# Second attention: scores made twice instead of turned probabilities, and row statistics by ScalarE's accumulators

## The chip, the core and the metric

One core of a Trainium2 chip. The metric is the device time of one execution in microseconds. The kernel is written engine by engine with explicit semaphores: TensorE (matmuls and transposes), VectorE, ScalarE, GpSimd and SyncE (which issues most DMAs) each run their own list of instructions in order.

## The reference, cut to what matters

`x` is 8 x 512 x 512, the context 8 x 120 x 512. Four layers follow each other, each added to `x`. The change is in the third, a cross attention with 16 heads of 32:

```python
x = x + _L0_xattn_ref(_layernorm(x, axis=-1), ctx_1024, ...)
x = x + _L0_ffn_ref(_layernorm(x, axis=-1), L0_ffn_rhs)
x = x + _L1_xattn_ref(_layernorm(x, axis=-1), ctx_1024, L1_xattn_w_q, L1_xattn_w_k, L1_xattn_w_v, L1_xattn_w_o)
x = x + _L1_ffn_ref(_layernorm(x, axis=-1), ...)

def _L1_xattn_ref(query, kv_source, w_q, w_k, w_v, w_o):
    q = (query @ w_q.T).reshape(B, T_q, N_HEADS, HEAD_DIM)
    k = (kv_source @ w_k.T).reshape(B, T_kv, N_HEADS, HEAD_DIM)
    v = (kv_source @ w_v.T).reshape(B, T_kv, N_HEADS, HEAD_DIM)
    scale = HEAD_DIM ** (-0.5)
    attn = jax.nn.softmax(jnp.einsum('bqhd,bkhd->bhqk', q, k) * scale, axis=-1)
    out = jnp.einsum('bhqk,bkhd->bqhd', attn, v).reshape(B, T_q, D_MODEL)
    return out @ w_o.T
```

## The kernel before

The 4096 rows are 32 tiles of 128 rows (`NT`), four tiles (`TB`) to a batch. `front` does the first two layers, `attention1` the third, `shared` and `experts` the fourth. Products are made in f16 with a high and a low half of each operand, three matmuls for one (`PASSES`); a high half is written by ScalarE (`..._high`), the low half by VectorE as the difference (`..._low`).

`attention1` is a software pipeline. In step t every engine works on several tiles, in an order that is written out by hand in its own `step(t)`. For a tile u: its own layer norm (`stats`, `aggregate` on VectorE, root and application on GpSimd), `rows_transposed`, `queries` in two halves, a store of the queries to memory (`q_rows`) and three loads that bring them back in another layout (`packed_queries`), `scores` for four chunks c of four heads each (128 rows of queries by 120 keys), `maximum`, `exps` (one Exp for each head with the negated maximum as bias and the row sum by the accumulator), `prob_transposed` (four f32 transposes a chunk), `prob_high` and `prob_low`, `outputs` (the weighted sums, 12 matmuls of 32 columns a chunk), `weighted` (times the inverse row sums), `output_transposed`, `product` (the output projection in two halves of six matmuls), `residual`, the norm of the next layer (`lg`: `gate_stats`, GpSimd's root and application), `gate_transposed`, `gate_high`, `gate_low` and `gate_logits`.

`scores` uses banks 1 and 2 of PSUM in turn, `prob_transposed` 3 and 4, `outputs` 5. Bank 6 is shared by `product` (`ps_y`) and `gate_transposed` (`ps_g`), bank 7 by the row and output transposes and the gate logits. For the shared bank 6, `product(u, 0)` waits `need(pe, s["g_lo"], u - 1)`, which is the low half of the gate transposes of tile u - 2, and `gate_transposed(u)` waits `need(pe, s["x_new"], min(u + 2, NT))`, the residual of tile u + 1. Both waits stand in both kernels. In step t these are `product(t - 3)` behind `gate_low(t - 5)`, and `gate_transposed(t - 4)` behind `residual(t - 3)`.

The last front steps and the first attention steps are woven by the table `JOIN` (which front step a half step of the attention stands behind), the last attention steps and the first pieces of the next layer by `TAIL`. In the lists of rows, L1421 is `scores`, L1435 `prob_transposed`, L1450 `outputs`, L1456 the transposes of rows, outputs and gate rows, L121 the queries, L1503 `product`, L1523 and L1525 `gate_logits`; L1353 is `exps`, L1343 `prob_high`, L1221 `maximum`, L1227 `prob_low`, L1283 `output_low`, L1299 `gate_low`, L1288 `residual`, L1235 and L1242 statistics and aggregate; L1147 is the q_rows store and L130 the loads.

## Time and profile before

| | before |
|---|---|
| median of 3 runs | 1251.64 us (1249.28 to 1256.03) |
| span of the profiled execution | 1257.6 us |
| TensorE busy | 1189.3 us (95%) |
| VectorE busy | 950.4 us (76%) |
| ScalarE busy | 708.7 us (56%) |
| GpSimd busy | 589.7 us (47%) |

The profiled execution is not one of the three timed ones; of it there is the span alone. The shares are of the whole span. The attention changed here fills about 270 to 560 us of it, so the stretches tell more than the shares. A matmul's length in the trace includes its way through the array: what one costs is the distance from its start to the next start.

### The profile page before, as it was taken

Reading aid. Unit: us, or ns where it says so; the run is one execution under the profiler, and the core shown is the slowest. Engines: PE = TensorE matmul, PEld = TensorE weight load, DVE = VectorE, ACT = ScalarE, POOL = GpSimd, SP = SyncE. Lnnn points to the kernel's source line nnn. Section 1 sums busy time; section 2 is a strip of 40 time slices with the busy share of each in tenths; the row PEclk is TensorE's granted clock in tenths of the full one; section 3 lists DMA queues with packets and bytes.
Section 4 is the critical chain, followed back from the end, with each engine's and each line's share of the span. In section 5 each row is a group of like instructions: output and inputs, shape, how many; then the busy total and the mean of one; then the engine's idle time right before and its main releaser. Section 6 shows DMA issues by size and latency. Waiting matters only on the chain.

```text
span 1257.6 us, 29419 instructions
## 1 busy us (share of the span) xinstructions
PE 1189.3 (95%) x10692; PEld 822.8 (65%) x10692; DVE 950.4 (76%) x2006; ACT 708.7 (56%) x1988; POOL 589.7 (47%) x685
## 2 busy tenths in 40 slices
PE   6888998799999999999999999999999998799996
PEld 3555665588888888786444445777777776466663
DVE  5889898899999999896677777777777775445460
ACT  4377788799899999896344322222222231365552
POOL 0047668737666667733200000445544345466744
PEclk9999999999999999999999999999999999899999
DMA  9522033134445454643870141221314320799987
GB/s 346 210 60 76 1 32 46 43 111 142 165 135 169 159 172 148 181 157 119 153 196 1 41 127 34 68 44 60 69 34 108 96 68 2 220 254 242 256 139 96
DMA packets 157567, 150.28 MB, mean 119 GB/s; under 512 B 78544, under 2 KB 111472, under 8 KB 157424
## 3 DMA queue, kind: packets, MB, share of 16 engines
q1 hardware_dynamic: 139584, 125.94, 35.5%
q0 software_dynamic: 13248, 21.15, 8.9%
q10 hardware_dynamic: 4592, 1.32, 0.6%
q8 instruction: 86, 1.41, 0.5%
q14 instruction: 57, 0.47, 0.1%
HBM read 84.93 MB, written 57.19 MB: 113 GB/s over the span
## 4 chain that ended last, share of the span: by engine, by line
PE 59%; DMA 17%; issue 8%; DVE 8%; POOL 5%; ACT 3%; ACTq 0%; SPq 0%; POOLq 0%; DVEq 0%
PE bank L121 28%; DMA lists<-att_land 14%; PE bank L1503 6%; PE bank L2125 5%; PE bank L955 4%; POOL lists L1629 4%; PE bank L1435 4%; PE bank L1456 3%; PE bank L1450 2%; PE bank L1421 2%; DMA q_rows<-att_land 1%; PE bank L1024 1%; ACT att_land L1353 1%; PE bank L872 1%; PE bank L891 1%
## 5 line engine op out<-in xcount | busy, mean ns | idle before, releaser
L1629 POOL DMA_INDIRECT lists<-att_land x128 | 134.4, 1050 | 310.7 <-DVE att_land L1770 166.8
L1353 ACT ACTIVATE att_land<-bank,att_land 128x120 f32<-128x120 f32 x512 | 178.3, 375 | 11.3 <-DVE att_land L1221 11.2
L2125 PE MATMUL bank<-att_land 128*128 128x512 f16 x768 | 177.3, 381 | 0.6 <-DVE program_logits L1304 0.6
L1952 ACT ACTIVATE att_land<-program_x 128x512 f32<-128x512 f32 x40 | 25.2, 631 | 195.2 <-DVE program_x L2094 165.1
L2125 PEld LDWEIGHTS bank<-att_land 128*128 128x128 f16 x768 | 75.4, 98 | 82.9 <-issue 2.0
L121 PE MATMUL bank<-program_xs,program_wgu 128*128 128x512 f16 x576 | 128.7, 379 | 0.6 <-DVE att_land L1729 0.6
L1353 ACT ACTIVATION_READ_ACCUMULATOR att_land<-bank,att_land 128x1 f32 x512 | 112.8, 221 | 0.0
L121 PE MATMUL bank<-att_land 128*128 128x128 f16 (+1 forms) x1560 | 101.0, 221 | 0.5 <-DVE att_land L1278 0.5
L121 PEld LDWEIGHTS bank<-program_xs,program_wgu 128*128 128x128 f16 x576 | 56.2, 98 | 67.5 <-DVE att_land L1729 1.1
L1221 DVE TENSOR_REDUCE att_land<-bank 128x4 f32<-128x480 f32 x128 | 82.4, 644 | 20.5 <-PE bank L1421 20.1
L1503 PE MATMUL bank<-att_land 128*128 128x512 f16 x384 | 93.4, 379 | 0.0
L121 PEld LDWEIGHTS bank<-att_land 128*128 128x128 f16 x1560 | 91.1, 98 | 3.6 <-DVE att_land L1278 0.7
L1227 DVE TENSOR_TENSOR att_land<-bank,att_land 120x512 f16<-120x512 f32 x128 | 86.9, 679 | 3.5 <-ACT att_land L1343 3.1
L1343 ACT ACTIVATE att_land<-bank 120x512 f16<-120x512 f32 x128 | 77.8, 610 | 19.0 <-PE bank L1435 15.7
L2132 PE MATMUL bank<-program_x 128*128 128x256 f16 x720 | 85.1, 273 | 0.0
L2294 POOL DMA_INDIRECT out_rows<-program_x,att_land x40 | 64.7, 1617 | 35.5 <-ACT program_x L2335 25.4
L121 PE MATMUL bank<-program_x 128*128 128x256 f16 (+2 forms) x504 | 80.5, 318 | 0.6 <-DVE program_x L2387 0.6
L1903 ACT ACTIVATE att_land<-att_land 128x512 f16<-128x512 f32 x64 | 40.2, 629 | 71.1 <-PE bank L2125 30.6
L1435 PE MATMUL bank<-program_ident,att_land 128*120 128x128 f32 x512 | 78.0, 275 | 1.4 <-DVE att_land L1227 1.4
L2132 PEld LDWEIGHTS bank<-program_x 128*128 128x128 f16 x720 | 70.4, 98 | 8.2
L428 POOL TENSOR_TENSOR program_x<-program_x,att_land 128x512 f32<-128x512 f32 x32 | 40.9, 1277 | 69.8 <-ACT att_land L546 69.8
L1435 PEld LDWEIGHTS bank<-program_ident,att_land 128*120 128x120 f32 x512 | 59.3, 138 | 13.7 <-issue 2.0
(305 smaller groups left out, 2817.2 us busy)
## 6 DMA issues: line engine op xcount, KB each, us to landing
att_land<-q_rows SPq DMA_DIRECT2D x96, 128.0 KB, 2.6
xn_rows<-att_land SPq DMA_DIRECT2D x37, 256.0 KB, 3.7
out_rows<-att_land SPq DMA_DIRECT2D x37, 256.0 KB, 6.4
q_rows<-att_land SPq DMA_DIRECT2D x32, 256.0 KB, 2.9
xt_tiles<-att_land SPq DMA_DIRECT2D x32, 256.0 KB, 2.1
x_rows<-program_x SPq DMA_DIRECT2D x8, 1024.0 KB, 4.8
att_land<-x_rows SPq DMA_DIRECT2D x8, 1024.0 KB, 5.6
program_xs<-xt_tiles SPq DMA_DIRECT2D x28, 256.0 KB
```

The lines of the kernel that those rows point to most:

```text
L121: last = pe.matmul(out, lhs(a, k), rhs(b, k), start=n == 0, stop=n == len(terms) - 1)
L955: last = pe.matmul(out, lhs, rhs, start=k == 0 and i == 0, stop=k == KC - 1 and i == 2)
L1221: dve.tensor_reduce(nmax[:, u % 2, c], ps_s[c % 2][:, :, :], AX.X, ALU.max, negate=True).then_inc(c4["max"], 1)
L1227: dve.tensor_tensor(pT[0:J, c, 1], ps_p[c % 2][0:J], pT[0:J, c, 0], ALU.subtract).then_inc(c4["p_lo"], 1)
L1343: act.activation(pT[0:J, c, 0], ps_p[c % 2][0:J], ACT.Copy).then_inc(c4["p_hi"], 1)
L1353: last = act.activation(prob[:, c, h, :], ps_s[c % 2][:, h, :], ACT.Exp, bias=nmax[:, u % 2, c, h:h + 1], accum_out=rsum[:, u % 2, n:n + 1])
L1435: last = pe.transpose(ps_p[c % 2][0:J, h, :], prob[:, c, h, :], g.ident[:, :])
L1503: last = pe.matmul(ps_y[:, :], oT[:, u % 2, a, k, :], g.wo1[:, b, k, :], start=k == 0 and n == 0, stop=k == KC - 1 and n == 2)
L1629: pool.indirect_dma_start(out=io["lists"], out_offset=bass.IndirectOffsetOnAxis(ap=index[:, t, k:k + 1], axis=0), in_=load[:, t, k, :], in ...
L2125: last = pe.matmul(ps_y[i][:, :], hid[:, c % 2, a, i * P:(i + 1) * P], wd[:, q, c, :], start=c == 0 and n == 0, stop=c == NC - 1 and n == 2)
L2132: last = pe.matmul(out, lhs(a, k), rhs(q, k), start=n == 0, stop=n == len(terms) - 1)
L2294: pool.indirect_dma_start(out=io["out"], out_offset=bass.IndirectOffsetOnAxis(ap=lst[:, u * CT + n, 0:1], axis=0), in_=res[:, c, n, :], in ...
```

## The change

The probabilities are no longer made in rows and turned. The scores of a chunk are made a second time with the operands swapped (`turned_scores`: 120 keys by 128 rows), into the banks that the transposes used. The negated maxima (128 x 16) are turned by one small transpose (`maxima_transposed`), copied to f16 by ScalarE (`maxima`) and brought by one DMA into a 97th row of the packed queries, against a row of ones in the keys, so that the product already holds score minus maximum. The Exp then runs on a whole chunk, once into f16 (the high half) and once in place in PSUM (`exps`), and `prob_low` takes the difference. The row sums come out of the weighted sums as a 33rd column of each head, for which the high half of the values has a column of ones (`g.vh`); head 0 has its own place in bank 7 and its own reciprocal (`inverse_sum0`) and scaling on ScalarE (`first_weighted`). The packed queries have three places instead of two. `output_high`, `output_low`, `gate_high` and `gate_low` stand half a step to a step later, and the order of all engines in a step is new.

For tiles 8 to 31, the sum of a row and the sum of its squared differences come from two ScalarE activations with accumulators (`row_sum`, `row_squares`), with three tiny GpSimd instructions, instead of VectorE's statistics and aggregate.

The core of the diff:

```diff
-    spread(sp, g.queries[:, u % 2], io["q_rows"][u], (0, 0, 1), done[u % 2])
+    spread(sp, g.queries[:, u % 3], io["q_rows"][u], (0, 0, 1), done[u % 2])
...
     LEAD, LAG = 6, 5
-    PLACE = (1, 0, 2, 3)
     SM = 7 * D + KC * HC * J
     HEAD = 5
-    ln = Norm(m, "b", g.early(0, [P, 2, D]))
+    PLACE = (1, 0, 2, 3)
+    SUMMED = 8
+    MAXROW = slice(3 * DH, 3 * DH + 1)
+    ROWS = slice(0, 3 * DH + 1)
+    ln = Norm(m, "b", g.early(7 * D, [P, 2, D]))
+    unused = g.early(9 * D, [P, 2, D], f16)
+    nmT = g.early(10 * D, [P, 2, P], f16)
     xT = g.early(2 * D, [P, 2, 2, KC, P], f16)
     qT = g.early(4 * D, [P, 2, KC, P], f16)
-    nmax = g.early(SM, [P, 2, KC, HC])
-    prob = g.early(7 * D, [P, 4, HC, J])
+    nmax = g.early(SM, [P, 2, HC, KC])
...
+            v = t - 5
+            if live(v):
+                sp.wait_ge(s["g_lo"], v + 1)
+                sp.dma_start(io["xt_tiles"][v, :, :], gT[:, v % 2].rearrange("p q k n -> p (q k n)")).then_inc(gt_out[v % 2], 16)
             u = t + 1
             if live(u):
                 sp.wait_ge(s["q_hi"], u + 1)
                 sp.wait_ge(s["q_lo"], u + 1)
                 sp.dma_start(io["q_rows"][u], qT[:, :, :, :].rearrange("p q k n -> p q (k n)")).then_inc(q_out[u % 2], 16)
+            r = t - 1
+            if live(r):
+                sp.wait_ge(s["n_ok"], r + 1)
+                need(sp, c4["t_mm"], KC * (r - 2))
+                to = g.queries[MAXROW, r % 3].rearrange("p r n -> p (r n)").rearrange("p (a n) -> p a n", n=P)
+                sp.dma_start(to, nmT[0:HEADS, r % 2, :]).then_inc(n_in[r % 2].handle, 16)
+            if live(u):
+                sp.wait_ge(q_out[u % 2], 16 * (u // 2 + 1))
+                need(sp, c4["t_mm"], KC * (u - 2))
+                need(sp, c4["s_mm"], KC * (u - 2) + 1 if u >= 2 else 0)
+                if u == 0:
+                    sp.wait_ge(f.a["sim"], NT)
+                packed_queries(sp, g, io, u, q_in)
             v = t - 4
             if live(v):
                 sp.wait_ge(lg.ok, v + 1)
                 sp.dma_start(io["xn_rows"][v * P:(v + 1) * P, :], lg.xn[:, v % 2]).then_inc(rows_out[v % 2], 16)
...
+        def mean(u):
+            if live(u) and u >= SUMMED:
+                i = u % 4
+                if u == SUMMED:
+                    pool.wait_ge(ln.aggr, SUMMED)
+                pool.wait_ge(ln.stats, u + 1)
+                pool.wait_ge(ln.ok, u - 3)
+                pool.tensor_tensor(ln.mv[:, i, 0:1], ln.st[:, i, 0:1], g.inv_d[:, :], ALU.mult).then_inc(ln.aggr, 1)
+
+        def summed_root(u):
+
+            i = u % 4
+            need(pool, squares, u + 1)
+            pool.tensor_tensor(ln.mv[:, i, 1:2], ln.st[:, i, 1:2], g.inv_d[:, :], ALU.mult).then_inc(varied.handle, 1)
+            need(pool, varied, u + 1)
+            pool.tensor_tensor(ln.ve[:, i], ln.mv[:, i, 1:2], g.eps[:, :], ALU.add).then_inc(ln.var, 1)
+            pool.wait_ge(ln.var, u + 1)
+            pool.tensor_tensor(ln.rstd[:, i], ln.ve[:, i], g.half[:, :], ALU.pow).then_inc(ln.root, 1)
...
+        def inverse_sum0(u):
+            if live(u):
+                dve.wait_ge(c4["o_mm"], KC * u + 2)
+                need(dve, of0, u - 1)
+                dve.reciprocal(rinv[:, u % 2, 0:1], ps_o0[:, DH:DH + 1]).then_inc(inv0.handle, 1)
...
-            maximum(t - 1, 3)
-            prob_low(t - 1, 0)
+            prob_low(t - 2, 1)
+            output_low(t - 3)
+            gate_low(t - 5)
             query_low(t + 1)
             rows_low(t + 2)
             yield
-            prob_low(t - 1, 1)
             maximum(t, 0)
+            logits(t - 5)
+            prob_low(t - 2, 2)
+            maximum(t, 1)
+            if t + 5 < SUMMED:
+                aggregate(ln, t + 5)
+            if t + 6 < SUMMED:
+                stats(ln, t + 6)
+            first_rows(t + 3)
+            prob_low(t - 2, 3)
+            inverse_sum0(t - 2)
+            maximum(t, 2)
+            inverse_sums(t - 2)
             weighted(t - 2)
-            logits(t - 5)
-            maximum(t, 1)
-            prob_low(t - 1, 2)
+            prob_low(t - 1, 0)
             residual(t - 3)
+            maximum(t, 3)
             gate_stats(t - 3)
-            maximum(t, 2)
-            aggregate(ln, t + 5)
-            stats(ln, t + 6)
-            first_rows(t + 3)
-            prob_low(t - 1, 3)
-            output_low(t - 2)
             aggregate(lg, t - 3)
-            gate_low(t - 4)
-            inverse_sums(t - 1)
...
+            act.activation(pT[0:J, c, 0], ps_p[c % 2][0:J], ACT.Exp)
+            act.activation(ps_p[c % 2][0:J], ps_p[c % 2][0:J], ACT.Exp).then_inc(c4["exp"], 1)
+
+        def row_sum(u):
+            if live(u) and u >= SUMMED:
+                if u == SUMMED:
+                    act.wait_ge(ln.stats, SUMMED)
+                act.wait_ge(f.q["x_new"], u + 1)
+                act.wait_ge(ln.aggr, u - 3)
+                if u > SUMMED:
+                    need(act, squares, u - 1)
+                act.activation(unused[:, u % 2], g.x[:, u, :], ACT.Copy, accum_out=ln.st[:, u % 4, 0:1]).then_inc(ln.stats, 1)
+
+        def row_squares(u):
+
+            if live(u) and u >= SUMMED:
+                act.wait_ge(ln.aggr, u + 1)
+                act.wait_ge(ln.var, u - 3)
+                act.activation(unused[:, u % 2], g.x[:, u, :], ACT.Square, scale=-1.0, bias=ln.mv[:, u % 4, 0:1],
+                               accum_out=ln.st[:, u % 4, 1:2]).then_inc(squares.handle, 1)
+
+        def maxima(u):
+            if live(u):
+                act.wait_ge(s["n_mm"], u + 1)
+                need(act, n_in[u % 2], 16 * (u // 2))
+                act.activation(nmT[0:HEADS, u % 2, :], ps_n, ACT.Copy).then_inc(s["n_ok"], 1)
...
-            prob_high(t - 1, 0)
+            exps(t - 2, 1)
+            output_high(t - 3)
+            gate_high(t - 5)
             query_high(t + 1)
             rows_high(t + 2)
             yield
-            prob_high(t - 1, 1)
-            exps(t - 1, 3)
-            prob_high(t - 1, 2)
-            exps(t, 0)
-            exps(t, 1)
-            prob_high(t - 1, 3)
-            output_high(t - 2)
-            gate_high(t - 4)
-            exps(t, 2)
+            exps(t - 2, 2)
+            maxima(t - 1)
+            exps(t - 2, 3)
+            row_squares(t + 5)
+            row_sum(t + 6)
+            first_weighted(t - 2)
+            exps(t - 1, 0)
...
+        def maxima_transposed(u):
+            if live(u):
+                pe.wait_ge(c4["max"], KC * u + KC)
+                need(pe, s["q_lo"], min(u + 3, NT))
+                pe.transpose(ps_n, nmax[:, u % 2].rearrange("p h c -> p (h c)"), g.ident[:, :]).then_inc(s["n_mm"], 1)
+
+        def turned_scores(u, c):
+
             if not live(u):
                 return
+            b = u // TB
+            if c == 0:
+                need(pe, n_in[u % 2], 16 * (u // 2 + 1))
             if u == 0 and c == 0:
+                need(pe, row_ok, 1)
                 pe.wait_ge(f.a["p_lo"], NT)
+            if u == TB and c == 0:
+                need(pe, row_ok, 2)
             if u == 0 and c == 1:
                 pe.wait_ge(f.a["y_ok"], NT)
-            pe.wait_ge(c4["exp"], KC * u + c + 1)
             need(pe, c4["p_lo"], KC * u + c - 1)
             for h in range(HC):
-                last = pe.transpose(ps_p[c % 2][0:J, h, :], prob[:, c, h, :], g.ident[:, :])
-            last.then_inc(c4["p_mm"], 1)
+                last = pe.matmul(ps_p[c % 2][0:J, h, :], g.keys[ROWS, b % 2, h, c * J:(c + 1) * J],
+                                 g.queries[ROWS, u % 3, h, c * P:(c + 1) * P], start=True, stop=True)
+            last.then_inc(c4["t_mm"], 1)
...
-            outputs(t - 2, 0)
-            outputs(t - 2, 2)
-            prob_transposed(t - 1, 0)
-            scores(t - 1, 3)
-            outputs(t - 2, 3)
+            queries(t + 1, 1)
             rows_transposed(t + 2)
-            prob_transposed(t - 1, 1)
+            turned_scores(t - 2, 2)
             scores(t, 0)
             yield
             product(t - 3, 0)
-            prob_transposed(t - 1, 2)
+            maxima_transposed(t - 1)
             gate_logits(t - 5)
+            turned_scores(t - 2, 3)
+            scores(t, 1)
+            outputs(t - 2, 1)
             queries(t + 2, 0)
-            scores(t, 1)
+            outputs(t - 2, 0)
+            scores(t, 2)
+            outputs(t - 2, 2)
+            outputs(t - 2, 3)
+            turned_scores(t - 1, 0)
             product(t - 3, 1)
-            prob_transposed(t - 1, 3)
-            outputs(t - 1, 1)
+            turned_scores(t - 1, 1)
+            scores(t, 3)
             output_transposed(t - 2)
-            scores(t, 2)
             gate_transposed(t - 4)
-            queries(t + 2, 1)
...
-        'tensor': [63, 65, 67, 67, 70, 71]}
+        'tensor': [65, 66, 67, 68, 70, 71]}
```

What this does to the order, on the two engines whose waits matter for each other. VectorE, around `gate_low` (L1299 before, L1353 after). The lines before the change are, from the top: `maximum(t, 2)`, aggregate and statistics of the own norm, `prob_low(t - 1, 3)`, `output_low(t - 2)`, aggregate of the gate norm, `gate_low(t - 4)`, the reciprocals, and the next step's `maximum`, `prob_low`, `query_low`, `rows_low`:

```order
L1221 TENSOR_REDUCE att_land<-bank 128x4
L1242 BN_AGGR attention_b_mv<-attention_b_st 128x2
L1235 BN_STATS attention_b_st<-program_x 128x6
L1227 TENSOR_TENSOR att_land<-bank,att_land 120x512
L1283 TENSOR_TENSOR att_land<-bank,att_land 128x512
L1242 BN_AGGR attention_g_mv<-attention_g_st 128x2
L1299 TENSOR_TENSOR att_land<-bank,att_land 128x512
L1261 RECIPROCAL att_land<-att_land 128x16
L1221 TENSOR_REDUCE att_land<-bank 128x4
L1227 TENSOR_TENSOR att_land<-bank,att_land 120x512
L1254 SCALAR_TENSOR_TENSOR att_land<-bank,att_land 128x512
L1278 TENSOR_TENSOR att_land<-bank,att_land 128x512
```

After the change, from `prob_low(t - 1, 0)`: `residual(t - 3)`, `maximum(t, 3)`, statistics and aggregate of the gate norm, and then the next step's `prob_low`, `output_low`, `gate_low`, `query_low`:

```order
L1276 TENSOR_TENSOR att_land<-bank,att_land 120x512
L1342 SCALAR_TENSOR_TENSOR program_x<-bank,program_x 128x512
L1270 TENSOR_REDUCE att_land<-bank 128x4
L1284 BN_STATS att_land<-program_x 128x6
L1291 BN_AGGR att_land<-att_land 128x2
L1276 TENSOR_TENSOR att_land<-bank,att_land 120x512
L1337 TENSOR_TENSOR att_land<-bank,att_land 128x512
L1353 TENSOR_TENSOR att_land<-bank,att_land 128x512
L1303 SCALAR_TENSOR_TENSOR att_land<-bank,att_land 128x512
```

The gate's low half stood at the end of the step, ahead of the next step's first instructions; now it stands behind the next step's first two, and the residual and the last maximum stand shortly ahead of it.

TensorE, from the gate transposes (into bank 6) to the first half of the output projection (L1503 before, L1608 after, into bank 6 too). Before:

```order
L1456 MATMUL bank_6<-program_ident,att_land 128x128 x4
L121 MATMUL bank_0<-att_land 128x128 x24
L1450 MATMUL bank_5<-att_land 128x32 x24
L1435 MATMUL bank_3<-program_ident,att_land 120x128 x4
L1421 MATMUL bank_2<-att_land 128x120 x4
L1450 MATMUL bank_5<-att_land 128x32 x12
L1456 MATMUL bank_7<-program_ident,att_land 128x128 x4
L1435 MATMUL bank_4<-program_ident,att_land 120x128 x4
L1421 MATMUL bank_1<-att_land 128x120 x4
L1503 MATMUL bank_6<-att_land 128x512 x6
```

After:

```order
L1531 MATMUL bank_4<-att_land 120x128 x4
L1505 MATMUL bank_2<-att_land 128x120 x4
L1562 MATMUL bank_7<-program_ident,att_land 128x128 x4
L1562 MATMUL bank_6<-program_ident,att_land 128x128 x4
L121 MATMUL bank_0<-att_land 128x128 x24
L1562 MATMUL bank_7<-program_ident,att_land 128x128 x4
L1531 MATMUL bank_3<-att_land 120x128 x4
L1505 MATMUL bank_1<-att_land 128x120 x4
L1608 MATMUL bank_6<-att_land 128x512 x6
L1513 MATMUL bank_0<-program_ident,att_land 16x128
```

Between the gate transposes and the projection stood 36 matmuls of weighted sums and two groups of probability transposes beside the queries; now the queries, one group of row transposes, one of turned scores (L1531) and one of scores are all that stands there.

## Rows read from the trace of the kernel before

**Rows 1.** Stretches: PE, PEld, DVE, ACT, POOL busy us (instructions), clock, DMA share, GB/s.

```profile
225.00:270.00 45.00, 35.84 (x480) 28.84 (x479) 38.20 (x85) 39.02 (x138) 26.16 (x40) 1.00 0.24 70
270.00:560.00 290.00, 286.97 (x4286) 248.32 (x4284) 268.82 (x528) 263.21 (x1076) 188.94 (x229) 1.00 0.49 157
560.00:612.00 52.00, 48.01 (x460) 30.27 (x459) 35.06 (x67) 29.87 (x105) 18.68 (x28) 1.00 0.45 159
```

**Rows 2.** Timeline of TensorE in one step: start, length, line, operation.

```profile
420.62 0.60 PE L1435 MATMUL bank<-program_ident,att_land 128*120 128x128 f32 x4
421.06 0.17 PE L1523 MATMUL bank<-att_land 128*128 128x18 f16 x1
...
421.26 1.50 PE L121 MATMUL bank<-att_land 128*128 128x128 f16 x24
422.60 0.38 PE L1421 MATMUL bank<-att_land 96*128 96x120 f16 x4
422.81 1.46 PE L1503 MATMUL bank<-att_land 128*128 128x512 f16 x6
...
424.54 0.46 PE L1450 MATMUL bank<-att_land 120*128 120x32 f16 x12
424.85 0.63 PE L1456 MATMUL bank<-program_ident,att_land 128*128 128x128 f32 x4
...
430.03 1.46 PE L1503 MATMUL bank<-att_land 128*128 128x512 f16 x6
431.33 0.60 PE L1435 MATMUL bank<-program_ident,att_land 128*120 128x128 f32 x4
```

**Rows 3.** Timeline of SyncE's DMA issues: q_rows stores and the loads behind one.

```profile
279.55 0.34 SPq L1147 DMA_DIRECT2D q_rows<-att_land  x1
...
409.22 0.34 SPq L1147 DMA_DIRECT2D q_rows<-att_land  x1
...
411.28 2.27 SPq L130 DMA_DIRECT2D att_land<-q_rows  x3
...
561.62 0.34 SPq L1147 DMA_DIRECT2D q_rows<-att_land  x1
```

**Rows 4.** The chain that ended last, two of its q_rows stores.

```profile
260.80 4.27 DMA q_rows<-att_land
...
332.99 7.44 DMA q_rows<-att_land
```

**Rows 5.** Timeline of ScalarE, 423 to 426 us.

```profile
423.70 0.36 ACT L1353 ACTIVATE att_land<-bank,att_land 128x120 f32<-128x120 f32 x1 [0.37 <-DVE att_land L1221]
...
424.05 0.35 ACT L1353 ACTIVATE att_land<-bank,att_land 128x120 f32<-128x120 f32 x1
...
425.06 0.61 ACT L1343 ACTIVATE att_land<-bank 120x512 f16<-120x512 f32 x1
425.54 0.62 ACT L1373 ACTIVATE att_land<-bank 128x512 f16<-128x512 f32 x1
```

**Rows 6.** Timeline of VectorE, 425 to 429 us.

```profile
425.03 0.69 DVE L1235 BATCH_NORM_STATS2 attention_g_st<-program_x 128x6 f32<-128x512 f32 x1
425.73 0.66 DVE L1221 TENSOR_REDUCE att_land<-bank 128x4 f32<-128x480 f32 x1
426.31 0.17 DVE L1242 BATCH_NORM_AGGREGATE attention_b_mv<-attention_b_st 128x2 f32<-128x6 f32 x1
...
427.56 0.68 DVE L1283 TENSOR_TENSOR att_land<-bank,att_land 128x512 f16<-128x512 f32 x1
428.16 0.17 DVE L1242 BATCH_NORM_AGGREGATE attention_g_mv<-attention_g_st 128x2 f32<-128x6 f32 x1
428.25 0.66 DVE L1299 TENSOR_TENSOR att_land<-bank,att_land 128x512 f16<-128x512 f32 x1
```

**Rows 7.** The chain of 197 to 300 us, its shares by line.

```profile
by line: PE bank L121 11.4%; issue 8.4%; PE bank L1503 7.6%; ACT att_land L1353 7.2%; DVE front_amax L768 5.3%; PE bank L1435 5.2%; PE bank L1024 4.4%; DMA q_rows<-att_land 4.1%; DVE att_land L790 3.9%; PE bank L1456 3.7%; PE bank L1450 3.4
```

**Rows 8.** A DMA issue: how many, KB each, median us to landing.

```profile
att_land<-in_gwT SPq DMA_DIRECT2D x1, 18.0 KB, 2.3
```

More of the change, by code:

```diff
@@ L212, in front @@
     rs0 = m.sb("rs0", [P, 8, 1])
-    eps4 = m.sb("eps4", [P, TB])
-    half4 = m.sb("half4", [P, TB])
-    gain4 = m.sb("gain4", [P, TB])
+    const4 = m.sb("const4", [P, 3, TB])
+    eps4, half4, gain4 = (const4[:, n] for n in range(3))
     xT = g.late(0, [P, 2, 2, KC, P], f16)
@@ L337, in shape, with landed @@
         return (slice(0, J), slice(0, D)) if kind[0] == "v" else (slice(0, P), slice(0, NH))
+    def landed(kind):
+        rows, cols = shape(kind)
+        return ps_j[rows, cols].rearrange("p (h o) -> p h o", h=HEADS) if kind == "v1" else ps_j[rows, cols]
     SPLITS = ["L0_Wv", "L1_wvT", "L1_wkT", "L1_wqT", "L1_woT"]
@@ L518, in job_high @@
                 act.wait_ge(j_mm, counted(REAL, n))
-                act.activation(hi, ps_j[rows, cols], ACT.Copy, scale=1 / WS).then_inc(j_hi, 1)
+                act.activation(hi, landed(kind), ACT.Copy, scale=1 / WS).then_inc(j_hi, 1)
         def rows_high(u):
@@ L703, in job_low @@
             else:
-                dve.scalar_tensor_tensor(lo, ps_j[rows, cols], 1 / WS, hi, ALU.mult, ALU.subtract).then_inc(j_lo, 1)
+                dve.scalar_tensor_tensor(lo, landed(kind), 1 / WS, hi, ALU.mult, ALU.subtract).then_inc(j_lo, 1)
         def statistics(u):
@@ L1183, in apply @@
                                ALU.mult).then_inc(norm.ok, 1)
-        def step(t):
+        def mean(u):
[14 more added lines that the diff above has]
+            pool.tensor_tensor(ln.rstd[:, i], ln.ve[:, i], g.half[:, :], ALU.pow).then_inc(ln.root, 1)
+        def step(t):
+            mean(t + 5)
+            if t == 0:
+                pool.wait_ge(f.j_hi, f.jobs)
+                pool.wait_ge(f.j_lo, f.jobs)
+                pool.memset(g.vh[:, :, :, DH:DH + 1], 1.0).then_inc(fixed.handle, 1)
             u = t - 4
@@ L2595, in program @@
         g.eps = m.sb("eps", [P, 1])
-        g.one = m.sb("one", [P, 1])
-        g.ws = m.sb("ws", [P, 1])
+        ones = m.sb("ones", [P, 3])
+        g.one, g.ws, g.inv_d = (ones[:, n:n + 1] for n in range(3))
         g.logits = m.sb("logits", [P, NT, E + 1])
@@ L2642, in program @@
             late = land[:, 6 * D + KN + QN + EARLY:6 * D + KN + QN + EARLY + LATE]
+            slots = land[:, 6 * D + KN:6 * D + KN + 3 * QN // 2]
             ends = 6 * D + KN + QN + EARLY + LATE
             g.v1 = g.land(ends, [P, 2, B, D], f16)
-            g.wo1 = g.land(ends + 8 * D, [P, 2, KC, D], f16)
+            g.vh = g.land(ends, [P, B, HEADS, DH + 1], f16)
+            g.vl = g.land(ends + 4 * D + VS, [P, B, D], f16)
+            g.wo1 = g.land(ends + 8 * D + VS, [P, 2, KC, D], f16)
             g.wd, g.res = g.land(ends, [P, 2, IS // P, D], f16), g.land(ends + 8 * D, [P, TB, D])
@@ L2648, in program @@
             g.keys = g.place[:, 0:KN].bitcast(f16).rearrange("p (s r n) -> p s r n", s=2, r=HC)
-            g.queries = g.place[:, KN:KN + QN].bitcast(f16).rearrange("p (s r n) -> p s r n", s=2, r=HC)
+            g.queries = slots.bitcast(f16).rearrange("p (s r n) -> p s r n", s=3, r=HC)
             g.simb, g.rs = g.place[:, KN:KN + JB], g.place[:, 2 * D:3 * D]
```

151 lines of the change are left out of this document (80 added, 71 removed).

## Prediction

> **What bounds the kernel now.** I read the busy times by stretch first, then the order and spacing of each engine inside one step, then the DMAs. The second attention runs in its pure form from about 270 to 560 us of the span. There TensorE is busy 286.97 of 290 us at full clock (1.00, the 2.4 GHz level), VectorE 268.8, ScalarE 263.2 and GpSimd 188.9 [rows 1]. The reader is to see that three engines are nearly full at once, so that work taken from one of them is worth only what the other two allow.
>
> One step in this stretch is read from the start of one group of probability transposes (L1435, 420.62) to the same group one step later (431.33): 10.71 us [rows 2]. TensorE's groups follow each other without a gap, so their spacings add up to the step: 24 query matmuls 1.34 us (421.26 to 422.60), four score matmuls 0.21, six output-projection matmuls 1.30, four f32 probability transposes 0.44, twelve weighted-sum matmuls 0.31, and a group of gate logits 0.20. TensorE therefore sets the step. The mean step is a little longer: the q_rows stores of tiles 5 and 31 start at 279.55 and 561.62, which is 282.07/26 = 10.85 us [rows 3]. The 0.14 of difference, 3.6 us over 26 steps, lies in a few steps in which the round trip of the queries through memory comes late (a store that took 7.44 us, [rows 4]).
>
> **What each part costs.**
>
> TensorE: 16 f32 transposes a tile go, 4 x 0.44 = 1.76 us. In their place stand 16 f16 matmuls of 97 rows and 128 columns. A f16 matmul of 128 columns costs 1.34/24 = 0.056 us, so four cost 0.22 and sixteen 0.89. The transpose of the maxima is one f32 transpose, 0.44/4 = 0.11. The 33rd column of the weighted sums I take at nothing: twelve of 32 columns take 0.31, 0.026 each, half of what 128 columns take, so it is not the columns that are paid there; the other end is 33/32 of 1.2 us, 0.04 us a step. Sum: 10.71 - 1.76 + 0.89 + 0.11 = 9.95 us a step.
>
> ScalarE: 16 Exp instructions a tile with their accumulator reads go (0.35 from one Exp to the next, read included, [rows 5]), and four copies of 0.49. Eight activations of 120x512 come, which I price like the copy of that shape, L1343: 0.60 us long, the next one 0.48 later [rows 5]. From tile 8 on come two activations of 128x512 with an accumulator, at 0.5 to 0.85 each, and two small ones of 0.2 to 0.25. ScalarE falls from 9.7 us a step (263.2 of 290) to 9.7 - 5.4 - 2.0 + 3.9 + 1.4 + 0.4 = 8.0 at most. Its chain for one chunk of a head group shortens too, and it is no longer near the bound.
>
> VectorE: the statistics and aggregate of the attention's own norm go (0.58 + 0.09), a one-column reciprocal and the wait for the second reciprocal come (0.1 to 0.3). Spacings of one instruction on it: 0.60 for a low half, 0.57 to 0.58 for a maximum, 0.70 for the gate norm's statistics, close to their whole length, 0.69, 0.09 for an aggregate [rows 6]. Its sum is near 9.6 us a step. GpSimd gets two tiny one-column instructions a step to its 188.9/290 x 10.71 = 7.0 us; its own idle time hides them. The copies of constants and tiles into other places cost nothing in a step.
>
> SyncE's queue gets one transfer a step, 16 pieces of 256 bytes, between the q_rows store and the loads of the same tile, and it waits there for ScalarE's copy of the maxima. Behind it stand the three q_rows loads, the xn_rows store, every fourth step the 1 MB x_rows store, then the weights. The loads wait for the landing of the store anyway, 2.06 us in the quiet row [rows 3], which is later than the maxima are ready (next parts), so the wait delays nothing behind it. The big stores and loads go out right behind the query loads, not right ahead of the q_rows store as before; that takes them from the path of the round trip.
>
> So engine sums would allow 9.95. But the order of the work makes a loop through three engines that is longer than any sum, and I take the step from it. The excerpts of the order above show it. Take the start of the first half of the output projection (L1608, writing bank 6) as zero:
>
> 1. TensorE reaches the first turned scores of the next tile behind the projection 1.30, the maxima's transpose 0.11, logits 0.20, turned scores 0.22, scores 0.21, weighted sums 0.31, queries 1.34, sums 0.31, scores 0.21 and sums 0.62: 4.83. They end 0.38 later (four matmuls of this length end 0.38 after their start, as L1421 in [rows 2]): 5.21.
> 2. ScalarE: hand-over 0.04, first Exp 0.48, second 0.60: 6.33.
> 3. VectorE, hand-over 0.03, then in its order: low half 0.60, residual 0.60, maximum 0.57, gate statistics 0.70, aggregate 0.09, low half 0.60, output's low half 0.60, gate's low half 0.66 to its end: 4.42, so 10.78.
> 4. The next projection waits for that gate low half (bank 6 is shared by the projection and the gate transposes, and the kernel waits for the gate low half of the tile two before). Hand-over 0.04: 10.82. The hand-overs are those of a few hundredths that stand between the end of one engine's instruction and the start of the next engine's in the rows (L1353 starting at 423.70 behind a maximum that was due, [rows 5]).
>
> In the kernel before, the same gate low half ends about 1.1 us ahead of the projection (428.91 against 430.03, [rows 2, 6]), since the gate transposes stand one query group earlier and the gate's halves at the end of the step, not behind the next one's start. I take 10.8 us. It leaves TensorE 0.85 us idle a step: half before the gate transposes, which wait for the residual, half before the projection.
>
> The Trainium skill, "ScalarE: Activation LUTs", section "Step-by-step: what each stage is for", says that ScalarE writes to PSUM with less latency than to SBUF; the second Exp writes to PSUM. No row of the kernel before shows such a write of this size. If it were worth 0.1 us, the loop would be 10.7 instead of 10.8.
>
> **The sum.** 26 steps at 10.80 instead of 10.85: -1.3 us. The rare late round trips are mostly covered now, since TensorE has slack in each step; what they cost new goes with the maxima (below), so I leave that at zero. In the overlap with the front (225 to 270 us) ScalarE is busy 39.0 of 45 us, and on the chain of 197 to 300 us its exps hold 7.2%, 7.4 us [rows 1, 7]. A chunk costs it 4 x 0.34 + 0.48 = 1.84 before and 1.08 after, so at most 0.4 of those 7.4, 3 us, can go; VectorE with 38.2 of 45 follows right behind. I take -2 (bounds -4 and +2, the latter if the new transfer stands in that chain). The tail (560 to 612, TensorE 48.0 of 52) has 4 us of idle time; the ticks of the next stage are moved by one or two half steps. I take 0, bounds -3 and +3. Sum -3.3: from 1251.6 to 1248. The profiled execution has a span of 1257.6, 6 us above the median of the three runs; in its own frame the sum gives 1254.3. About 0.5% (6 us) is what can be told from no change here.
>
> **The rivals.**
>
> The loop is shorter than worked out, and TensorE's 9.95 sets the step. For it: the loop rests on spacings read while all engines hammered PSUM; ScalarE has much less to do now. Against it: it must lose 0.85 us out of 10.8, of which half is TensorE's own certain time. Full effect: 26 x (9.95 - 10.85) - 2 = -25, so 1226; half of it (10.4) gives 1238.
>
> The maxima's transfer comes late (slower). It starts behind the maxima's transpose (end at 1.30 + 0.28), ScalarE's small copy (0.2 to 0.25) and a hand-over, at about 1.9 in the frame above, and TensorE wants it at 4.83. So it is hidden if it lands within 2.85 us. The nearest rows: the 18 KB load landed in 2.3 us, the q_rows store (256 KB) of 409.22 let its loads go at 411.28, 2.06 later, and the one of 260.80 took 4.27 [rows 3, 4, 8]. I take 2.3. It goes out behind a 256 KB store to the same queue, and is 16 pieces of 256 bytes into one partition. At 3.3 us the step becomes 11.25, 26 x 0.4 - 2 = +8, so 1260; at 3.7, 1270. It decides from about 3.2 us on. The same size of loss comes if the two Exps take 1.5 us instead of 1.08.
>
> The Trainium skill, "DMA: Bandwidth & Descriptors", section "Anatomy of one DMA — SWDGE (gpsimd) path", puts the fixed part of a transfer at about 2.0 us whatever its size. The store of 409.22, 2.06 us for 256 KB, agrees. By the page the maxima would land in time with 0.8 us to spare.
>
> That the change moves nothing at all because the engine that it frees was not the bound is the forecast's own core: ScalarE's relief is real and worth nothing in a step.
>
> **How the numbers follow.** Forecast (step of 10.65 to 11.0): 0.45, 1248, its own range 1241 to 1256. Loop clearly shorter: 0.30, 1224 to 1243. Transfer or Exps late: 0.25, 1256 to 1275. Cut so that two in ten are left out: 1226 to 1266. Faster by over 0.5% (below 1245.4) is the shorter loop and a little of the forecast, 0.33; slower (above 1257.9) 0.24; the rest 0.43.
>
> **What would show it.** In the steady stretch: q_rows stores 10.8 us apart; TensorE's projection (L1608) waiting for VectorE's L1353 and the gate transposes (L1562) waiting for L1342, about 0.4 us each a step; VectorE waiting for L1407 before the low half of chunk 0; ScalarE busy 7 to 8 us of a step; no wait of TensorE for the maxima's transfer. If L1531 waits for the DMA in most steps, the slower rival holds. If TensorE is busy again all the time and the step is under 10.4, the loop was mis-sized. The prediction would also be wrong if TensorE's clock fell once it idles; in the overlap it was at 1.00 with TensorE busy 35.8 of 45 us [rows 1].

## The result: 2.6% slower

The changed kernel takes 1285.5 us (median of the runs that count: 1285.48, 1282.69, 1285.55), the kernel before 1253.7; the ratio is 1.0258 with a 95% interval of 1.0214 to 1.0302. One execution of the changed kernel ran disturbed (1385.9 us) and is left out. The prediction was 1248 (1226 to 1266), with the same time as before as the likeliest outcome; the measured time lies 19.5 us above that range.

The profiled execution took 1285.48 us with a span of 1283.7. For the kernel before a second trace was taken beside the experiments (span 1249.1, time 1250.82). It is the better yardstick: the span of 1257.6 shown ahead of the prediction holds one wait of 12.5 us for gathered rows, far behind the attention, which the second trace does not have (see the experiments).

The stretches of the changed kernel that answer to [rows 1] (busy us and instructions of PE, PEld, DVE, ACT and POOL, then clock, DMA share, GB/s):

```profile
283.00:585.00 302.00, 270.95 (x4188) 222.93 (x4186) 259.43 (x494) 213.85 (x456) 196.96 (x274) 0.99 0.45 147
585.00:646.00 61.00, 48.13 (x503) 29.77 (x501) 34.06 (x70) 25.21 (x50) 15.47 (x22) 0.97 0.35 125
```

No engine is full any more. TensorE, busy 287 of 290 us before, idles 31 of 302. ScalarE has been relieved as planned (213.9 of 302), and the step did not fall for it. Where a chain of engines closes into a loop, busy times no longer tell the step.

SyncE's issues, as in [rows 3], the q_rows stores (the first one shown is that of tile 5, the last that of tile 31):

```profile
283.02 0.34 SPq L1166 DMA_DIRECT2D q_rows<-att_land  x1
...
408.72 0.32 SPq L1166 DMA_DIRECT2D q_rows<-att_land  x1
...
420.01 0.32 SPq L1166 DMA_DIRECT2D q_rows<-att_land  x1
...
584.74 0.32 SPq L1166 DMA_DIRECT2D q_rows<-att_land  x1
```

The undisturbed step is 11.29 us, predicted 10.8, before 10.71. Cut at these stores the difference of the spans, 1283.7 - 1249.1 = 34.6 us, falls into:

| stretch | before (second trace) | changed | difference |
|---|---|---|---|
| start to the store of tile 5 | 281.2 | 283.0 | +1.8 |
| tile 5 to tile 31 (26 steps) | 281.3 | 301.7 | +20.4 |
| tile 31 to the next layer's first token loads | 48.2 | 61.0 | +12.8 |
| from there to the end | 638.4 | 637.9 | -0.5 |

One step of TensorE in the changed kernel, as in [rows 2]:

```profile
419.79 1.46 PE L1608 MATMUL bank<-att_land 128*128 128x512 f16 x6
421.09 0.27 PE L1513 MATMUL bank<-program_ident,att_land 128*16 128x128 f32 x1
...
424.63 0.41 PE L1531 MATMUL bank<-att_land 97*120 97x128 f16 x4
424.88 1.46 PE L1608 MATMUL bank<-att_land 128*128 128x512 f16 x6
...
427.58 0.63 PE L1562 MATMUL bank<-program_ident,att_land 128*128 128x128 f32 x4 [0.36 <-issue]
428.05 1.50 PE L121 MATMUL bank<-att_land 128*128 128x128 f16 x24
430.18 0.63 PE L1562 MATMUL bank<-program_ident,att_land 128*128 128x128 f32 x4 [0.63 <-DVE att_land L1337]
430.65 0.39 PE L1531 MATMUL bank<-att_land 97*120 97x128 f16 x4
```

The L1562 at 427.58 is the gate transposes (bank 6), late by 0.5 us because of the residual (L1342 below, which ends at 427.48). The one at 430.18 is the row transposes (bank 7). They wait for VectorE's L1337, `output_low`, and not the projection for L1353, `gate_low`, as the prediction had it: the next projection follows at 431.08 without a wait. VectorE beside it, as in [rows 6], and ScalarE's two Exps of chunk 0:

```profile
425.08 0.60 ACT L1406 ACTIVATE att_land<-bank 120x512 f16<-120x512 f32 x1 [0.59 <-PE bank L1531]
425.57 0.59 ACT L1407 ACTIVATE bank<-bank 120x512 f32<-120x512 f32 x1
```

```profile
426.19 0.69 DVE L1276 TENSOR_TENSOR att_land<-bank,att_land 120x512 f16<-120x512 f32 x1 [0.43 <-ACT bank L1407]
426.80 0.68 DVE L1342 SCALAR_TENSOR_TENSOR program_x<-bank,program_x 128x512 f32<-128x512 f32 x1
427.40 0.65 DVE L1270 TENSOR_REDUCE att_land<-bank 128x4 f32<-128x480 f32 x1
427.96 0.68 DVE L1284 BATCH_NORM_STATS2 att_land<-program_x 128x6 f32<-128x512 f32 x1
428.68 0.18 DVE L1291 BATCH_NORM_AGGREGATE att_land<-att_land 128x2 f32<-128x6 f32 x1
428.78 0.66 DVE L1276 TENSOR_TENSOR att_land<-bank,att_land 120x512 f16<-120x512 f32 x1
429.36 0.68 DVE L1337 TENSOR_TENSOR att_land<-bank,att_land 128x512 f16<-128x512 f32 x1
429.95 0.68 DVE L1353 TENSOR_TENSOR att_land<-bank,att_land 128x512 f16<-128x512 f32 x1
```

The reader is to follow the loop once: projection 419.79, turned scores of the next tile 424.63 (4.84 behind), Exps 425.08 to 426.16, low half of chunk 0 at 426.19, six more instructions of VectorE up to the end of `output_low` at 430.04, row transposes at 430.18, turned scores, scores, projection at 431.08. 11.29 us.

The waits of TensorE from tile 5 to tile 31, in total, times, longest:

```profile
PE bank L1562 <- DVE att_land L1337: 18.8, 25, 3.7
PE bank L1562 <- issue: 9.1, 25, 0.4
PE bank L1531 <- DMA att_land<-att_land: 2.0, 6, 0.5
PE bank L1608 <- DVE att_land L1353: 0.8, 1, 0.8
```

### The profile page after: what moved, and what is told of

It is laid out like the page before. It is cut to its first block, busy times and chain, and to the rows that moved or that the text cites. A ratio compares the mean times of both kernels' runs of the same rounds, so it can differ in the third digit from the quotient of the medians.

```text
span 1283.7 us, 28783 instructions
## 1 busy us (share of the span) xinstructions
PE 1182.8 (92%) x10724; PEld 804.0 (63%) x10724; DVE 950.7 (74%) x1992; ACT 651.9 (51%) x1252; POOL 599.1 (47%) x735
## 4 chain that ended last, share of the span: by engine, by line
PE 73%; DVE 13%; issue 7%; ACT 3%; DMA 2%; POOL 1%; ACTq 0%; DVEq 0%; SPq 0%; POOLq 0%
PE bank L121 25%; PE bank L2238 14%; PE bank L2231 13%; PE bank L1608 4%; PE bank L958 4%; DMA att_land<-att_land 2%; DVE att_land L1276 2%; PE bank L1531 2%; PE bank L1027 2%; DVE att_land L1284 2%; PE bank L1562 2%; ACT bank L1407 2%; PE bank L1557 1%; DVE att_land L1337 1%; PE bank L1505 1%
## 5 line engine op out<-in xcount | busy, mean ns | idle before, releaser
L1276 DVE TENSOR_TENSOR att_land<-bank,att_land 120x512 f16<-120x512 f32 x128 | 87.2, 681 | 24.7 <-ACT bank L1407 23.1
L1608 PE MATMUL bank<-att_land 128*128 128x512 f16 x384 | 95.9, 386 | 5.3 <-DVE att_land L1353 5.3
L1562 PE MATMUL bank<-program_ident,att_land 128*128 128x128 f32 x384 | 59.6, 278 | 36.5 <-DVE att_land L1337 21.5
L1407 ACT ACTIVATE bank<-bank 120x512 f32<-120x512 f32 x128 | 76.2, 595 | 0.0
L1562 PEld LDWEIGHTS bank<-program_ident,att_land 128*128 128x128 f32 x384 | 40.3, 140 | 47.9 <-issue 43.6
L1897 POOL DMA_INDIRECT att_land<-xn_rows,att_land x40 | 42.4, 1061 | 55.1 <-DMA out_rows<-att_land 21.8
```

The costliest lines, as they stand in the source:

```text
L1276: dve.tensor_tensor(pT[0:J, c, 1], ps_p[c % 2][0:J], pT[0:J, c, 0], ALU.subtract).then_inc(c4["p_lo"], 1)
L1407: act.activation(ps_p[c % 2][0:J], ps_p[c % 2][0:J], ACT.Exp).then_inc(c4["exp"], 1)
L1562: last = pe.transpose(to[:, k, :], src[:, k * P:(k + 1) * P], g.ident[:, :])
L1608: last = pe.matmul(ps_y[:, :], oT[:, u % 2, a, k, :], g.wo1[:, b, k, :], start=k == 0 and n == 0, stop=k == KC - 1 and n == 2)
```

## Experiments

Theory A: a loop through TensorE, ScalarE and VectorE, closed by the row transposes (they wait for `output_low`, since output and row transposes share bank 7), sets the step. Theory B: the same loop, closed by `gate_low` and the projection (the prediction's). Theory C: VectorE is full or slowed. Theory D: the maxima's transfer sets it. All variants are of the changed kernel; e8, not in the table, is the kernel before once more. "Quiet step" is the shortest distance of two q_rows stores that keeps coming back. In most runs most steps have it; in e2 and e10 it is 5 and 7 of 26, in e5 and e9 7 and 6, and there the mean tells more. "Mean" is the distance from tile 5 to tile 31 over 26, "time" the median.

| run | quiet step | mean step | tail, tile 31 to loads | time |
|---|---|---|---|---|
| before (steps of the second trace) | 10.71 | 10.82 | 48.2 | 1253.7 |
| changed | 11.29 | 11.60 | 61.0 | 1285.5 |
| e1 output low half first | 10.99 | 11.31 | 62.8 | 1282.3 |
| e2 gate statistics later | 10.56 | 11.17 | 65.9 | 1283.3 |
| e3 chunk 0 later | 11.71 | 11.88 | 62.2 | 1297.0 |
| e4 chunk 3 later | 11.30 | 11.56 | 62.0 | 1292.5 |
| e5 all three moves | 10.27 | 10.99 | 68.3 | 1280.3 |
| e6 statistics early | 11.01 | 11.18 | 56.4 | 1273.9 |
| e7 statistics on VectorE | 11.30 | 11.52 | 61.1 | 1286.4 |
| e9 order | 10.27 | 10.79 | 57.6 | 1267.7 |
| e10 and offload | 10.27 | 10.94 | 59.6 | 1271.3 |
| e11 and statistics on VectorE | 10.93 | 11.12 | 58.0 | 1274.4 |

The step is read to 0.01 us and repeats within a trace; the times of a variant lie 3 to 13 us apart over its four runs. So the verdicts on the loop go by the step. The kernel before, run beside the variants, took 1252.9 (e1 to e4), 1249.4 (e5 to e7) and 1251.6 (e9 to e11).

**e1, one swap on VectorE.**

```diff
-            prob_low(t - 2, 1)
             output_low(t - 3)
+            prob_low(t - 2, 1)
             gate_low(t - 5)
```

> The changed kernel, with one swap on VectorE: the low half of the output (tile t-3) stands ahead of the low half of probabilities (t-2, chunk 1) at the start of a step. Nothing else moves and no work is added. Theory A (the loop closes over rows_transposed, which waits for output_low because both transposes use bank 7): the row transposes start 0.57 us earlier, then the gate's low half, whose time is not changed, binds the projection next; the step falls from 11.29 to about 11.0, 26 steps give -8 us. Theory B (the loop closes over gate_low and the projection, as the prediction had it): the gate's low half ends at the same time, step and time unchanged. Theory C (VectorE is simply full, or slowed by ScalarE's traffic on PSUM): unchanged.

The step fell to 10.99. A expected about 11.0, B and C no change:

```profile
410.01 0.33 SPq L1166 DMA_DIRECT2D q_rows<-att_land  x1
...
420.99 0.32 SPq L1166 DMA_DIRECT2D q_rows<-att_land  x1
```

As A expected, the gate's low half binds next: VectorE's L1353 ends at 431.30 and the projection starts at 431.45. The 26 steps gained 7.7 us. In the traced execution, 3.5 us longer than the changed kernel's, they are lost again: 4.9 us ahead of tile 5 (287.9 instead of 283.0), 1.7 in the tail and 4.6 behind it. The median time is 3.2 us lower, with runs from 1276.4 to 1289.0, so the time alone would show nothing.

**e2, the gate norm's statistics out of the loop.**

```diff
-            gate_stats(t - 3)
-            aggregate(lg, t - 3)
...
             logits(t - 5)
+            gate_stats(t - 4)
+            aggregate(lg, t - 4)
```

> The changed kernel, with the gate norm's statistics and aggregate moved on VectorE from the end of a step to behind the logits of the next one (the same instructions, for tile t-4 instead of t-3). Theories A and B (a loop of three engines): 0.8 us of work leave the loop, the step falls from 11.29 to about 10.5, 26 steps give -21 us, about 1264. Theory C (VectorE's sum): nothing is removed, no change within 3 us.

The quiet step is 10.56: the same instructions at another place are worth 0.73 us in such a step and 0.43 in the mean, which refutes C. The time hardly moved, 19 us above what was expected: the 26 steps are 11.3 us shorter, the tail is 4.9 longer, and 5.9 more stand behind the tail. In the steps with weight scaling GpSimd now comes late with the gate rows, steps of 11.5 us (TensorE's waits, 300 to 500 us):

```profile
PE bank L1562 <- issue: 6.9, 15, 1.2
PE bank L1562 <- POOL att_land L1204: 4.9, 9, 1.1
PE bank L1531 <- DMA att_land<-att_land: 2.6, 5, 0.8
```

**e3 and e4, the same 0.45 us of ScalarE work at two places.**

```diff
+            if c == 0 and u >= SUMMED:
+                act.wait_ge(c4["exp"], KC * u + c)
+                act.activation(again[:, :, :], g.x[:, u, 0:3 * P].rearrange("p (k n) -> p k n", k=3), ACT.Copy)
             act.activation(pT[0:J, c, 0], ps_p[c % 2][0:J], ACT.Exp)
```

(e4: `c == 3`.)

> The changed kernel, with one more ScalarE copy (128x384, SBUF to SBUF, result unused, about 0.45 us) in front of the two Exps of chunk 0, tiles 8 to 31. Theories A and B: chunk 0 is in the loop, so the step becomes 0.45 to 0.55 longer for 23 steps, +10 to +13 us, although ScalarE is idle some 4 us in each step. Theory C: ScalarE has the time, no change. A rival D (the maxima's transfer sets the step) expects no change either.

> The same added copy in front of the two Exps of chunk 3 instead, tiles 8 to 31. Theories A and B: chunk 3 is outside the loop, and VectorE waits 0.34 us behind its low half anyway, so 0 to +3 us. If more work on ScalarE costs time wherever it stands, +10 us as with chunk 0.

The copy is 0.52 long, and the Exp behind it starts 0.43 later. In front of chunk 0 it costs 0.42 us a step (11.71), in front of chunk 3 nothing (11.30). ScalarE is busy 72 and 74% of 290 to 580 us. That is the loop seen from ScalarE. It speaks against D too, which the waits above refute by themselves: TensorE waited 2.0 us in six waits for the transfer. The time of e4 is 7 us above the changed kernel's although its 26 steps are not longer; in its trace 5 us more stand ahead of tile 5 (its store at 288.1) and 5 behind the tail. The overlap with the front came out longer in seven traces (changed kernel and variants) than in the other four, with a later start of the first store (226 against 223). In six of the seven the granted clock of 200 to 300 us is 0.88, with tile 5 at 286.4 to 288.1; in the four it is 0.93, with tile 5 at 282.7 to 283.6. What makes the start late, no run tells.

**e5, three moves at once**: `output_low` and `gate_low` ahead of chunk 1's low half, statistics behind the logits, and the residual ahead of chunk 0's low half.

> The changed kernel, with three moves on VectorE together: output_low and gate_low ahead of the low half of chunk 1, the gate norm's statistics behind the next step's logits, the residual ahead of the low half of chunk 0. Theory A: every piece of VectorE work behind chunk 0 but one maximum leaves the loop, TensorE's own 9.95 is nearly reached in quiet steps (10.1 to 10.2). But the gate norm's statistics are then late for GpSimd, which has 5.9 us of weight scaling in every third step until step 24; as in the run before, the gate transposes wait for GpSimd there. Mean 10.7 to 10.9, about 1264. Theory C (VectorE's sum): no change from the changed kernel.

Quiet steps of 10.27: the loop no longer sets them. The mean is 10.99, a little above the expected 10.7 to 10.9, with TensorE waiting 13.2 us for GpSimd's L1204 (gate rows), as expected, and 2.7 us for the maxima. The time, 1280.3, missed the expected 1264 by 16 us: the 26 steps gained 15.9, but tile 5 came 4.1 later and the tail is 7.3 longer.

**e6, statistics early.** VectorE's order at the start of a step: `output_low`, `gate_low`, statistics, aggregate, `query_low`, chunk 1's low half, `rows_low`. The residual stands as in e5.

> The same, but the gate norm's statistics and aggregate stand directly behind gate_low at the start of the next step, and VectorE's order there is output_low, gate_low, statistics, aggregate, query_low, low half of chunk 1, rows_low. Theory A: the loop is as short as in the run above and GpSimd gets the aggregate 2 us earlier than there, so few waits for it: quiet steps 10.1 to 10.2, mean about 10.5, 26 steps give -28 us from the changed kernel, about 1255, the same as before the change. If the time is still that of the changed kernel, the steady stretch is not what costs.

A miss: 23 of the 26 steps are 11.0, and the time is 1273.9 where 1255 was expected. I had moved `rows_low` behind the statistics, and the gate logits (L1628) wait for it, since they too use bank 7:

```profile
430.39 0.17 PE L1628 MATMUL bank<-att_land 128*128 128x18 f16 x1 [0.67 <-issue]
```

VectorE's L1332 (`rows_low`) ran from 429.61 to 430.29. It is the mistake of the prediction once more: a wait on a shared bank that was not followed to its instruction. e9, with `rows_low` early again, has no such wait.

**e7, the second part of the change undone** (`SUMMED = NT`).

> The changed kernel without its second part: SUMMED = NT, so VectorE takes the statistics and aggregate of the attention's own norm for all 32 tiles, and ScalarE's two sums and GpSimd's two extra instructions go. Theory A: the 0.67 us stand in the middle of the step, where VectorE waits 0.34 and 0.43 us anyway, so the step grows by 0.0 to 0.2, +2 to +5 us. Theory C (VectorE is full): +0.67 a step, +15 us.

Step and time are those of the changed kernel (11.30; 1286.4 against 1285.5). Expected were +2 to +5 us by A and +15 by C. Taking the row statistics from VectorE is worth nothing here: VectorE does them in the middle of the step, where it waits.

**e8, the kernel before again.**

> The kernel before, unchanged, for a second trace. Between the last gate logits and the read-back of the routing lists it had 452 us, in five traces of the changed kernel and its variants 432 to 441, and TensorE waited 12.5 us there for the gathered rows. If that is the kernel's own (TensorE reaches that place earlier against the lists), the second trace shows 450 us and the wait again; if it is chance of the transfers, it can show 435 and little wait.

The lists were read back 435.3 us behind the last logits (1045.2 against 609.9), and TensorE did not wait. So the 452 us of the first trace and its wait of 12.5 us are not the kernel's own.

**e9, the order mended.**

```diff
-            prob_low(t - 2, 1)
             output_low(t - 3)
             gate_low(t - 5)
+            prob_low(t - 2, 1)
             query_low(t + 1)
             rows_low(t + 2)
+            gate_stats(t - 4)
+            aggregate(lg, t - 4)
...
+            residual(t - 3)
             prob_low(t - 1, 0)
-            residual(t - 3)
             maximum(t, 3)
-            gate_stats(t - 3)
-            aggregate(lg, t - 3)
```

> As the run with all moves out of the loop, but the gate norm's statistics and aggregate stand behind rows_low (0.7 us earlier for GpSimd), and rows_low stays early enough for the gate logits, which share bank 7 with the row transposes (the fault of the run before with its step of 11.01). Theory A: quiet steps 10.1 to 10.3, some waits for GpSimd in the steps with weight scaling, mean 10.7, about 1262. If bank 7 was not what held the step at 11.01, it stays near 11.

Quiet steps 10.27, mean 10.79, 1267.7 us: the best variant, 6 us above what was expected and still 1.3% above the kernel before beside it (1251.6; interval of the ratio 1.0087 to 1.0176). Its 26 steps take 280.5 us, those of the kernel before 281.3. What is left to the kernel before stands in the overlap (tile 5 at 287.0 against 281.2) and in the tail (57.6 against 48.2).

**e10, e11: GpSimd relieved, then VectorE loaded.** Both have the order of e9. The f16 copy of the scaled weights moves to ScalarE, one step later, and GpSimd's low half of it a step later too; e11 adds `SUMMED = NT`.

> The same, and the f16 copy of the scaled weights (1.89 us of GpSimd every third step) goes to ScalarE one step later, with the low half a step later too. If GpSimd is the next bound: its waits vanish, mean step 10.2 to 10.4, 8 us less than the run above, about 1253, as before the change. If not, same time as the run above.

> The same as the run above, with the attention norm's statistics on VectorE for all tiles (SUMMED = NT). Now that TensorE sets the step and VectorE has little idle time left, 0.67 us more on VectorE should cost: step 10.4 to 10.6, +5 us against the run above. If it is still free there, VectorE has more room than its order suggests.

e10 missed: GpSimd's waits did vanish, but now the maxima's transfer is the next to be late, 8.0 us in ten waits where e9 had 3.8 in eleven:

```profile
PE bank L1535 <- DMA att_land<-att_land: 8.0, 10, 1.9
PE bank L1566 <- DVE att_land L1337: 3.1, 1, 3.1
```

Its 26 steps are 3.9 us longer than those of e9, not 8 us shorter.

In e11 TensorE's weighted sums wait for VectorE's low halves (L1276) in most steps (waits of 290 to 570 us):

```profile
PE bank L1561 <- DVE att_land L1276: 11.5, 21, 0.6
```

Every step but the last two is at least 10.92, where e10 has 7 of 26 near 10.27; in the last two no statistics are left to make, and they are 10.28 and 10.27. The whole cost is smaller than the 0.67 us a step that VectorE does more: 4.5 us over the 26 steps (0.17 in the mean, since e10 loses 8.0 us to the transfer where e11 loses 1.8) and 3.1 us in the time, against 5 expected. So once the loop is opened, VectorE has no room for 0.67 us more, and the second part of the change gets some worth.

No version beat the kernel before; the interval nearest to it is that of e9.

## Why the prediction was wrong

The prediction's sum was -3.3 us, and the spans differ by +34.6 (second trace of before). By its own terms the miss is: overlap -2, measured +1.8; the 26 steps -1.3, measured +20.4; tail 0, measured +12.8. Of the 21.7 us missed in the 26 steps 12.7 are step 4 of the loop (26 x (11.29 - 10.80)) and 8.2 the rare late steps; the other 0.8 is the first trace's mean step, 10.85 where the second has 10.82. With step 4 at its measured size alone the forecast would have been 1261, slower but inside the range. What carried the time out of it is step 4 together with the rare late steps, the tail and the overlap. Step 4 is shown by experiments; the others are read from the traces.

**TensorE's sum: right.** Predicted 9.95. The groups of the changed step add up to 10.0 (11.29 less 0.50 and 0.79 of waiting). Four turned scores took 0.22 to 0.25, the maxima's transpose 0.11, and twelve weighted sums 0.31 as before, so the 33rd column cost nothing.

**ScalarE: right.** Exp and second Exp are 0.49 apart and 0.59 long, as priced. The first, writing f16 to SBUF, is 0.60 long, the second, writing f32 to PSUM, 0.59. ScalarE was busy 8.0 us of a step (213.9 of 302), as worked out. The Trainium skill, "ScalarE: Activation LUTs", section "Step-by-step: what each stage is for", calls PSUM the destination with the lower latency; the 0.1 us that the prediction tried for it does not show here.

**Steps 1 to 3 of the loop: right, to some hundredths.** Turned scores 4.84 behind the projection (4.83), VectorE's low half at 6.40 (6.36), `output_low` beginning at 9.57 (9.52).

**Step 4: this one failed.** It took the gate's low half as what closes the loop, 10.82. I had the list of waits of the row transposes and did not follow it: `rows_transposed(t + 2)` waits for `need(pe, s["o_lo"], u - 4)`, tile t - 3, and that low half had moved from the end of the step to the start of the next, just like the gate's. It is 0.60 earlier on VectorE than `gate_low`, but the row transposes stand 0.90 ahead of the projection on TensorE (0.47 + 0.22 + 0.21). With the hand-over, 0.14 instead of 0.04, 11.29. e1 shows it: with that low half one place earlier the step is 10.99, and then the gate's low half binds, as the prediction had it. Even that loop is 0.17 longer than its 10.82, of which 0.11 is the hand-over to TensorE (0.15 instead of 0.04).

**The rare late steps: wrong, at zero.** They were put at nothing because TensorE's slack would cover them. The steps beside the quiet one cost 8.2 us now (301.7 less 26 x 11.29) and 2.8 before. Most are the steps with the 1 MB store or the weights, 0.4 to 0.6 each, and the step in which ScalarE fetches the next layer's tokens, 3.4 and 1.6 behind it.

**The overlap: wrong sign, -2.** It was +1.8 here and up to +7 in the variants. ScalarE's relief is there (65.8 us busy between 200 and 300 us, 87.2 in the first trace of before), but TensorE is busy 78.0 of these 100 us, before 84.9 and 85.4, and its granted clock is lower: 0.93, against 1.00 and 0.98 in the two traces of before. The rows show what the lower level costs, the same four matmuls at the 2.4 and at the 1.2 GHz level (granted clock 0.88 in 245 to 250 us and 0.50 in 250 to 255):

```profile
247.50 1.02 PE L1027 MATMUL bank<-att_land 128*128 128x512 bf16 x4 [2.63 <-DVE att_land L793]
...
250.79 1.89 PE L1027 MATMUL bank<-att_land 128*128 128x512 bf16 x4 [0.94 <-ACT att_land L568]
...
253.34 2.59 PE L121 MATMUL bank<-att_land 128*128 128x128 f16 x24
```

24 query matmuls take 2.59 us here and 1.50 in the step above. What first makes TensorE late in the overlap stays open.

**The tail: +12.8, taken as 0 with bounds of 3.** The prediction saw that the pieces of the next layer move by one or two half steps and gave no reason why that should cost nothing. TensorE idles 12.9 of 61.0 us, before 4.0 of 48.2. The first of these pieces comes at 615.5, 31 us behind the last q_rows store, before 12.7 behind it (575.2 against 562.5): `TAIL` puts it a step later, behind the last maxima's transpose, which uses the same bank 0. Until then there is little to fill the waits. The largest of them in the tail is the very one that the prediction had for the steady stretch, the projection behind the gate's low half (560 to 650 us):

```profile
PE bank L1608 <- DVE att_land L1353: 5.3, 3, 2.3
```

The projections there start at 584.2, 594.9 and 607.9, and the granted clock was 0.66 between 600 and 605 us. This is read from the traces; no run took the tail alone. e6 and e9 gave back 4.6 and 3.4 us of it. A shorter loop does not do that by itself: in e2 and e5, where the gate statistics come latest, the tail is 4.9 and 7.3 us longer than the changed kernel's, with 8.0 us of waits for GpSimd's L1204 in each.

**The slower rival, the maxima's transfer: not it.** It cost 2.0 us in all. From issue to landing it took 2.6 us in the median (1.6 to 3.7), where the prediction took 2.3 and allowed 2.85 (its own 1.9 and 4.83 allow 2.93). It becomes a bound only at a step near 10.3 (e10).

**The second part of the change** I had as hidden for ScalarE and GpSimd, and as a relief of VectorE that the loop does not use. e7 shows that: undone, the step stays at 11.30.

## What to carry to other kernels

When steps of a software pipeline are reordered, list for every instruction that moved to a later place who waits for it, also through a shared PSUM bank, and close each of these loops by hand; two candidates stood 0.3 us a step apart (11.29 and 10.99), and only the shorter had been worked out. Engine sums told 9.95 and busy shares did not tell the step. Moving 0.8 us of statistics out of the loop was worth 0.73 us in a quiet step (e2), removing 0.67 us of other statistics outside it nothing (e7). But the step is not all: with the loop opened and the 26 steps as short as before (e9), the kernel was still 1.3% slower, in the overlap and the tail. Work out fill and drain as terms of their own; here they held 14.6 of the 34.6 us.

## What was not expected of the chip

TensorE can fall back from the full clock in the middle of a kernel, in a stretch in which it is busy most of the time: with TensorE busy 33.1 of 45 us (230 to 275 us) the granted clock was 0.50 to 0.93 in six of nine slices of 5 us. In the second trace of before, busy 36.5, it was below 1.00 in one of nine (0.66), though TensorE was busy only 2.7 and 3.1 of 5 us in two slices in a row at 1.00. Which waits cost the clock, these rows do not tell. And a single trace of the kernel before held a wait of 12.5 us that the next one did not have, as much as the whole tail costs here.
